# State-space stage with one chained step-size product, a tap and the masks on ScalarE, normalisation scaling inside the loop, and the first drive on VectorE

## The reference

```python
x = jnp.einsum('ed,bld->bel', in_proj_w, hidden_states)       # 256 channels, from ctx_1024
xc = conv(pad(x, 3), conv_w)                                  # 4 taps along the tokens, per channel
u = jax.nn.silu(xc + conv_b[None, :, None])
x_dbl = jnp.einsum('ke,bel->bkl', x_proj_w, u)
dt_lo, Bm, Cm = x_dbl[:, :8], x_dbl[:, 8:24], x_dbl[:, 24:]
delta = jax.nn.softplus(jnp.einsum('er,brl->bel', dt_proj_w, dt_lo) + dt_proj_b[None, :, None])
A = -jnp.exp(A_log)                                           # 256 channels x 16 states
def step(state, xs):
    dA = jnp.exp(d_t[..., None] * A)
    state = state * dA + (d_t * u_t)[..., None] * B_t[:, None, :]
    return state, jnp.einsum('ben,bn->be', state, C_t)
y = (scan(step) + D[None, :, None] * u) * jax.nn.silu(z)      # z = layernorm(x)
x = x + jnp.tanh(g_xattn[0]) * y
```

## Time and profile before

| what | us |
|---|---|
| median of three runs | 1066.79 |
| the profiled execution, its own time | 1067.51 |
| its span | 1065.8 |
| first convolution instruction on VectorE | 12.00 |
| B rows sent to DRAM (line 275); first row DMA back (line 280) issued | 29.39; 31.29 |
| first instruction of the series | 34.20 |
| delta complete; POOL's second du starts | 52.04; 52.11 |
| first scan | 56.90 |
| last product of the loop ended | 169.93 |
| last addition of the stage ended | 177.03 |
| blank tile (`blank`, a memset on POOL, line 405) set | 1.16 |

### The profile page before, as it was taken

How to read it: one execution, slowest core, us unless ns; L and a number is a source line. 1 busy time by engine, 2 the same in 40 slices (tenths; PEclk the granted TensorE clock), 3 DMA queues, 4 the chain that set the end, 5 groups by cost and what they waited for, 6 DMA issues and landing times. The chain is left out here.

```text
span 1065.8 us, 16398 instructions
## 1 busy us (share of the span) xinstructions
PE 846.5 (79%) x5192; PEld 502.3 (47%) x5198; DVE 735.5 (69%) x1433; ACT 575.6 (54%) x1095; POOL 398.9 (37%) x337
## 2 busy tenths in 40 slices
PE   3446565899999999999499588999649999925587
PEld 1112223563477777777267473333425666622235
DVE  5889998688976667666678777997361324138685
ACT  3433433468777777777366365888413433215462
POOL 0376660037655555454133163000003676310132
PEclk8679998999999999999789899999959999966589
DMA  3212202900000000000000100410194332240001
GB/s 95 81 68 71 79 20 87 347 11 2 15 20 16 20 16 20 20 15 10 6 1 1 55 1 2 141 41 2 45 333 133 78 74 46 35 114 1 0 1 40
DMA packets 44346, 57.61 MB, mean 54 GB/s; under 512 B 5672, under 2 KB 35120, under 8 KB 44288
## 3 DMA queue, kind: packets, MB, share of 16 engines
q1 hardware_dynamic: 37792, 48.72, 13.7%
q0 software_dynamic: 4416, 6.03, 3.4%
q10 hardware_dynamic: 2080, 2.10, 0.6%
HBM read 50.29 MB, written 6.49 MB: 53 GB/s over the span
## 5 line engine op out<-in xcount | busy, mean ns | idle before, releaser
L1237 POOL TENSOR_TENSOR a_scratch<-a_scratch,a_inverse 128x512 f32<-128x512 f32 x64 | 66.6, 1041 | 115.2 <-DVE a_inverse L1373 115.2
L324 PE MATMUL bank<-ssm_seen,ident 128*128 128x512 f32 x128 | 63.8, 622 | 38.8 <-DVE ssm_seen L500 38.8
L392 ACT ACTIVATE bank<-ssm_delta,ssm_a_neg 128x510 f32<-128x510 f32 x64 | 44.1, 690 | 80.7 <-DVE ssm_state L490 77.7
L426 POOL TENSOR_TENSOR ssm_drive<-ssm_du,ssm_b_row 128x1024 f32<-128x1024 f32 x32 | 75.2, 2351 | 33.4 <-DVE ssm_state L490 33.4
L2436 PE MATMUL bank<-wup,moe_xT 128*128 x184 | 83.0, 594 | 1.2 <-ACT moe_xT L2499 1.1
L2230 DVE TENSOR_REDUCE a_tops<-bank 128x4 f32<-128x1024 f32 x64 | 77.7, 1223 | 8.6 <-PE bank L1912 5.6
L490 DVE TENSOR_TENSOR_SCAN ssm_state<-bank,ssm_drive 128x512 f32<-128x512 f32 x64 | 74.8, 1210 | 7.5 <-POOL ssm_drive L426 4.9
L2671 DVE TENSOR_TENSOR moe_act_f<-bank,moe_silu 128x512 f32<-128x512 f32 x23 | 15.9, 691 | 90.9 <-ACT moe_silu L2506 79.1
L2080 ACT ACTIVATE wup<-bank,a_exp_scale 128x1024 f32<-128x1024 f32 x64 | 71.2, 1114 | 13.6 <-PE bank L1935 13.6
L1156 ACT ACTIVATE a_scratch<-bank,a_bias,a_q_factor 128x256 f32<-128x256 f32 x128 | 71.1, 560 | 7.1 <-DVE a_bias L1360 6.8
L968 PE MATMUL bank<-keys,a_scratch 128*128 (+1 forms) x256 | 69.1, 392 | 1.6 <-DVE xn L1300 0.7
(11 more groups left out here) (477 smaller groups left out, 2186.3 us busy)
## 6 DMA issues: line engine op xcount, KB each, us to landing
ssm_b_row<-ssm_b_spill SPq DMA_DIRECT2D x16, 512.0 KB, 3.6
wup<-in_l_up_dram SPq DMA_DIRECT2D x8, 1024.0 KB, 8.3
a_wq_in<-in_l1x_q_dram SPq DMA_DIRECT2D x32, 128.0 KB, 2.1
wdn<-in_l_down_dram SPq DMA_DIRECT2D x8, 512.0 KB, 9.5
keys<-in_l1x_o_dram SPq DMA_DIRECT2D x1, 2048.0 KB, 10.8
X<-in_x_dram SPq DMA_DIRECT2D x1, 1024.0 KB, 7.0
lora_raw<-in_l_gate_dram SPq DMA_DIRECT2D x1, 1024.0 KB, 8.3
lora_raw<-in_l_up_dram SPq DMA_DIRECT2D x1, 1024.0 KB, 10.3
```

The lines of the kernel that those rows point to most:

```text
L324: last = pe.matmul(bank[:, 4 + 2 * k + h, :], core.ident[:, :], seen[:, k, h * HALF:(h + 1) * HALF], start=False, stop=m >= STEPS - CC, sk ...
L426: pool.tensor_tensor(drive[:, k, :], du[:, k, :], b_row[:, n % NROW, :], ALU.mult).then_inc(S["drive_ready"], 1)
L1237: pool.tensor_tensor(prob[:, j, :, :], prob[:, j, :, :], inverse[:, j, :].unsqueeze(2).to_broadcast([P, 2, SEQ]), ALU.mult).then_inc(S["p_ ...
```

## The change

- The transposed first step-size matrix is multiplied by the second on TensorE (lines 310 and 315 of the new kernel), and the 256 x 256 product is applied to u directly (`steps_in`). 32 rows are made from u instead of 40, behind it.
- Dummy matmuls on the blank tile are placed before the first real ones and between the small ones (`keep_busy`).
- ScalarE writes the last tap straight from the bank into `ssm_conv`; VectorE adds the other three, reading the bank. `ssm_padded` is gone.
- The mask is ScalarE's Relu(1/16 - small), four bytes wide, in place of POOL's one-byte comparison.
- The C rows are spread in float32: 32-row `x_rows` by a float32 `select`, two products of two passes each. The split into parts is gone.
- The normalisation keeps its statistics ahead of the loop. Its root is exp(-0.5 log), x is centred by ScalarE inside the loop, and the scale is applied in the silu, one piece per 128 tokens.
- VectorE makes du(0) and drive(0); POOL makes du(1) and drives 1 to 31.
- The input DMAs are waited for in smaller groups, and ident and select go ahead of x. The last additions are 512 wide, four instead of eight.

The core of the diff:

```diff
-        w_dt2 = s.sb("w_dt2", [XR, CC * P])
+        w_dt2, w_xT = s.sb("w_dt2", [DR, CC * P]), s.sb("w_xT", [DR, CC * P])
+        w_c = s.sb("w_c", [P, CC, CC * P])
...
-        select3 = s.sb("select3", [96, NS * P], BF16)
-        padded = s.sb("padded", [P, CC, NB, SEQ + PAD])
+        select_in, select = s.sb("select_in", [2 * NS, NS * P], BF16), s.sb("select", [2 * NS, NS * P])
+        sixteenth, nmean, log_var = s.sb("sixteenth", [P, 1]), s.sb("nmean", [P, NT]), s.sb("log_var", [P, NT])
...
+        DT_BANK = (0, 6)
...
-                sp.dma_start(w_in[:, :], d["l0x_in"]).then_inc(S["w_s"], 16)
-                sp.dma_start(ctxT[:, :], d["ctxT"]).then_inc(S["w_s"], 16)
+                sp.dma_start(w_in[:, :], d["l0x_in"]).then_inc(S["in_s"], 16)
+                sp.dma_start(ctxT[:, :], d["ctxT"]).then_inc(S["in_s"], 16)
...
+                sp.dma_start(w_dt2[:, :], d["l0x_dt2"]).then_inc(S["w_s"], 16)
+                sp.dma_start(core.ident[:, :], d["ident"]).then_inc(S["ident_s"], 16)
+                sp.dma_start(select_in[:, :], d["select3"][0:2 * NS, NS * P:2 * NS * P]).then_inc(S["s_s"], 16)
+                sp.dma_start(core.X[:, :, :], d["x"].rearrange("(t p) d -> p t d", p=P)).then_inc(S["x_s"], 16)
...
-                pe.wait_ge(S["w_s"], 4 * 16)
-                for k in range(CC):
+                def keep_busy(n):
+                    for _ in range(n):
+                        pe.matmul(bank[:, 7, 0:DM], core.blank[:, 0:P], core.blank[:, :], start=True, stop=True)
...
+                def steps_in(o, k):
+                    for h in range(2):
+                        last = pe.matmul(bank[:, DT_BANK[o] + h, :], w_c[:, k, o * P:(o + 1) * P],
+                                         u[:, k, h * HALF:(h + 1) * HALF], start=k == 0, stop=k == CC - 1,
+                                         skip_group_check=True)
+                    if k == CC - 1:
+                        last.then_inc(S["dt_done"], 1)
+
+                pe.wait_ge(S["blank_set"], 1)
+                keep_busy(5)
+                pe.wait_ge(S["in_s"], 2 * 16)
+                for k in range(CC):
+                    in_proj(k)
+                pe.wait_ge(S["w_s"], 2 * 16)
+                pe.wait_ge(S["ident_s"], 16)
+                for k in range(CC):
+                    last = pe.transpose(bank[0:DR, 4, k * P:(k + 1) * P], w_x[:, k, 2 * NS:XR], core.ident[:, :])
+                last.then_inc(S["x_turned"], 1)
+                keep_busy(3)
+                pe.wait_ge(S["w_xT_ready"], 1)
+                for k in range(CC):
+                    last = pe.matmul(bank[:, 5, k * DM:(k + 1) * DM], w_xT[:, k * P:(k + 1) * P], w_dt2[:, :],
+                                     start=True, stop=True)
+                last.then_inc(S["chained"], 1)
+                keep_busy(4)
+                pe.wait_ge(S["w_c_ready"], 1)
+                for k in range(CC):
+                    pe.wait_ge(S["u_ready"], k + 1)
+                    for o in range(CC):
+                        steps_in(o, k)
...
+                        last = pe.matmul(bank[0:2 * NS, 4 + h, :], w_x[:, k, 0:2 * NS], u[:, k, h * HALF:(h + 1) * HALF],
                                          start=k == 0, stop=k == CC - 1)
                 last.then_inc(S["rows_done"], 1)
+                pe.wait_ge(S["diag_ready"], CC)
                 pe.wait_ge(S["rows_ready"], 1)
                 for k in range(CC):
-                    for h in range(2):
-                        last = pe.matmul(bank[:, 2 * k + h, :], w_dt2[2 * NS:XR, k * P:(k + 1) * P],
-                                         x_rows[2 * NS:XR, h * HALF:(h + 1) * HALF], start=True, stop=True)
-                    last.then_inc(S["dt2_done"], 1)
-                pe.wait_ge(S["diag_ready"], CC)
-                pe.wait_ge(S["parts_ready"], 1)
-                for k in range(CC):
+                    if k == CC - 1:
+                        pe.wait_ge(S["positive_ready"], CC)
                     for h in range(2):
                         pe.matmul(bank[:, 4 + 2 * k + h, :], skip_diag[:, k, :], u[:, k, h * HALF:(h + 1) * HALF],
                                   start=True, stop=False, skip_group_check=True)
-                pe.wait_ge(S["s_s"], 2 * 16)
-                pe.wait_ge(S["abs_done"], CC)
-                pe.wait_ge(S["positive_ready"], CC)
+                pe.wait_ge(S["select_ready"], 1)
 
                 def c_rows(n):
                     if n >= 1:
                         pe.wait_ge(S["seen_ready"], CC * n)
                     for h in range(2):
-                        last = pe.matmul(bank[:, 2 + h, :], select3[:, n * P:(n + 1) * P],
-                                         parts[:, h * HALF:(h + 1) * HALF], start=True, stop=True)
+                        last = pe.matmul(bank[:, 2 + h, :], select[:, n * P:(n + 1) * P],
+                                         x_rows[:, h * HALF:(h + 1) * HALF], start=True, stop=True)
...
+                def tap(k):
                     act.wait_ge(S["in_done"], k + 1)
-                    for h in range(2):
-                        last = act.copy(padded[:, k, 2 * h:2 * h + 2, PAD:PAD + SEQ],
-                                        bank[:, 2 * k + h, :].rearrange("p (b n) -> p b n", b=2))
-                    last.then_inc(S["pad_ready"], 1)
-                for k in range(CC):
+                    act.activation(two(conv[:, k, :]), bank[:, 2 * k:2 * k + 2, :], ACT.Identity,
+                                   scale=conv_w[:, k, TAPS - 1:TAPS]).then_inc(S["tapped"], 1)
+
+                def input_of(k):
                     act.wait_ge(S["conv_done"], k + 1)
                     act.activation(u[:, k, :], conv[:, k, :], ACT.Silu, bias=conv_b[:, k, :]).then_inc(S["u_ready"], 1)
-                act.wait_ge(S["set_up"], 2)
-                s.norm_root(act)
-                act.wait_ge(S["rows_done"], 1)
-                act.copy(two(x_rows[:, :]), bank[0:XR, 4:6, :]).then_inc(S["rows_ready"], 1)
-                act.wait_ge(S["rows_ready"], 1)
-                act.copy(parts[0:2 * NS, :], x_rows[0:2 * NS, :]).then_inc(S["parts_hi"], 1)
-                act.wait_ge(S["w_s"], 4 * 16)
+
+                act.preload_act_table_set("silu_and_others")
...
+                act.wait_ge(S["x_turned"], 1)
+                act.copy(w_xT[:, :], bank[0:DR, 4, 0:CC * P]).then_inc(S["w_xT_ready"], 1)
+                act.wait_ge(S["chained"], 1)
+                act.copy(w_c[:, :, :], bank[:, 5, :].rearrange("p (k n) -> p k n", k=CC)).then_inc(S["w_c_ready"], 1)
+                input_of(0)
+                act.wait_ge(S["s_s"], 16)
+                act.copy(select[:, :], select_in[:, :]).then_inc(S["select_ready"], 1)
+                input_of(1)
...
+                    act.activation(is_small[:, k, :], small[:, k, :], ACT.Relu, scale=-1.0, bias=sixteenth[:, 0:1]
+                                   ).then_inc(S["small_known"], 1)
...
+                for k in range(CC):
+                    exponential(k)
+                logarithm(0)
+                act.wait_ge(S["rows_done"], 1)
+                act.copy(two(x_rows[:, :]), bank[0:2 * NS, 4:6, :]).then_inc(S["rows_ready"], 1)
+                positive_part(0)
+                logarithm(1)
+                positive_part(1)
+                act.wait_ge(s.aggr_done, NT)
+                act.activation(log_var[:, :], core.meanvar[:, :, 1], ACT.Ln, bias=core.eps[:, 0:1]).then_inc(S["logged"], 1)
+                act.wait_ge(S["logged"], 1)
+                act.activation(core.rstd[:, :], log_var[:, :], ACT.Exp, scale=-0.5).then_inc(S["root"], 1)
...
+                def centre(t):
+                    act.activation(core.xn[:, t, :], core.X[:, t, :], ACT.Identity, bias=nmean[:, t:t + 1]
+                                   ).then_inc(S["centred"], 1)
+
+                act.wait_ge(S["nmean_ready"], 1)
                 for m in range(STEPS):
                     decays(m)
-                act.wait_ge(s.xn_ready, NT)
-                act.activation(silu_z[:, :, :], core.xn[:, :, :], ACT.Silu).then_inc(S["silu_z_done"], 1)
-                act.wait_ge(S["gates_s"], 2 * 16)
+                    if m >= CC * NT and m % CC == 0:
+                        centre(m // CC - NT)
+                act.preload_act_table_set("silu_and_others")
+                act.wait_ge(S["root"], 1)
+                for t in range(NT):
+                    act.wait_ge(S["centred"], t + 1)
+                    act.activation(silu_z[:, t, :], core.xn[:, t, :], ACT.Silu, scale=core.rstd[:, t:t + 1]
+                                   ).then_inc(S["silu_z_done"], 1)
...
-                for k in range(CC):
-                    pool.wait_ge(S["e_ready"], k + 1)
-                    pool.tensor_scalar(is_small[:, k, :], small[:, k, :], 1.0 / 16, None, ALU.is_lt).then_inc(S["small_known"], 1)
-                for k in range(CC):
-                    pool.wait_ge(S["delta_ready"], k + 1)
```

(30 more changed lines are left out.)

109 lines of the change are left out of this document (50 added, 59 removed).

## The result

The changed kernel took 1057.67 us, the median of 7 runs (1053.64 to 1061.38); the kernel before took 1066.79 beside it (7 runs, 1065.38 to 1071.86). The ratio is 0.989 (0.987 to 0.991). The profiled execution took 1053.64 us with a span of 1051.6, where such an execution was forecast at 1052.8 with a span near 1051.1. So the forecast of the gain held for that execution to within 0.8 us, and the median of seven fell 5.6 us short of it, 0.3 us inside the range's end at 1058.

A forecast was written before the change was run, and what follows sets the result against it. The state-space stage was bounded by an engine-hopping preparation chain, then by VectorE in the loop. Savings of 3.0 + 1.6 + 7.2 + 3.1 + 0 - 0.4 + 0.2 = 14.7 us gave 1052.1 against the 1066.79 median, range 1048 to 1058.

The forecast's parts named there:

- rivals 3 and 4: Loop: C rows late at the high level, about 1056.5, chance 0.09; preparation: TensorE low, +5 us, 1057, chance 0.07.
- Start to convolution: From kernel start to VectorE's convolution: dummies and a covered table load start it at 9.0 against 12.00, saving 3.0 us.
- rival 4: Preparation: TensorE stays at the low level and the dummies stand in the way, +5 us, 1057; chance 0.07.
- Convolution: VectorE's convolution: two multiplies leave, six multiply-adds reading a bank take 7.85 us, done at 16.85; saves 1.6 us.
- Convolution to series: Convolution's end to the step-size series: fewer passes and no copy, 5.5 us against 12.73; saves 7.2 us.
- Series: VectorE's step-size series: POOL's masks and first du leave that stretch, 3.7 us back, 0.6 us wait; saves 3.1 us.
- First drive: Series' end to the first scans: VectorE and POOL take turns on shared ports, so 0 us gained (-2.1 to +2.4).
- rival 1: First drive: ports cost more than thought, POOL goes first and VectorE's du(0) waits; minus 2.1 us, 1054.2; chance 0.13.
- rival 2: First drive: no port conflict, so the drive gain is real; +2.4 us, 1049.7; chance 0.14.
- Tail: After the loop to the stage's end: four wide additions for eight, silu pieces hidden; saves 0.2 us (-0.3 to +0.5).
- Loop: State-space loop: f32 C rows cost nothing at the high level, only the first pair runs late; -0.4 us (-1.5 to 0).
- rival 5: Loop: f32 C rows at TensorE's low level, +3.1 us per pair, +47 over 15 pairs, 1099; chance 0.03.

## Why the prediction was right or wrong

**Inside its range, short by 5 us.** 1052.1 was forecast, 1048 to 1058; the 13 runs have 1057.2. The direction and most of the mechanism held, term by term up to the first scan. That the median lies inside the range owes something to luck: it is 0.8 us from the end, and it lies near rivals 3 and 4 (1056.5 and 1057) although neither of them happened.

*Start to convolution:* 12.00 - 9.06 = 2.9 us (3.0). Without dummies 1.1 of it is lost, and 3.1 more further on, since the passes behind silu then run longer too. The run without dummies is rival 4, made real: 4.2 us, priced at 5.

*Convolution:* 7.71 us for six multiply-adds reading banks (7.85); done at 16.77, forecast 16.85.

*Convolution to series:* 22.32 - 16.77 = 5.55 us, 5.5 forecast. Undoing the product of the matrices alone costs 4.7 us of the 7.2. The rest of the term is put down to the covered table load and to the level by subtraction; the run without dummies shows that the level is worth up to 3.1 us here.

*Series:* 14.30 us long, 14.75 forecast: the wait for the positive part was 0.17, not 0.6. The four-byte mask costs next to nothing (1.37 and 1.29 us; 1.30 and 1.29 with one byte). Of the 3.7 us, putting the masks back on POOL loses 1.2 and putting du(0) back 2.0 (16.32 us long for 14.30).

*First drive:* turns, as forecast. The first scan came 4.44 us behind the series (4.8), the first product 8.92 against 61.46 - 52.04 = 9.42 before. So about +0.4 us, where 0 was said; neither rival 1 nor rival 2 happened. Taking du(1) from POOL gave 0.7 more; the two together are far from the 2.4 on paper.

*Tail:* the eight silu pieces cost nothing that a wait shows; the tail's two products wait for the last gather, as before. What comes behind the stage has the same length.

*Loop: the step that failed.* The term was -0.4, from a rule that at the high level nothing is late and that only the first pair meets the low one. The first half nearly holds: no product waits for a C row in the 128-row runs behind the first pair, only the last product is 0.35 us late. The second half is what failed. Against the low level in the loop (rival 5) the prediction argued that the stretch was granted 0.95 with TensorE 60% busy "and the change makes it busier". It did become busier, and the conclusion is wrong: the loop is 86% busy and granted 0.85. The seven profiled executions with 32-row f32 C rows and no fill took 122.2, 123.7, 127.6, 128.0, 122.2, 128.1 and (kernel before with such rows) 128.5 us for it, at 0.81 to 0.87. Those with all rows in use, 96 rows in bf16, or one bf16 pass took 120.1 to 121.0. So the loop lost 2 to 8 us by execution, the unexplained 0.5 included. The level is low in pieces, and that is why rival 5's 47 us did not come: a stretch makes a product late only if it falls on a C row or leaves TensorE behind, and the gather has time until two steps later. In the four executions near 128 us three things came together: the level rose only 12 to 13 us after the first gather had begun (after 3.5 us in the first profile), so that the first C row ran low; two of the later low stretches were 7 us long; and the last low stretch left the gathers late for the last product, which waited 1.9 to 2.5 us.

How this makes the 5 us: in the first profile the loop and its tail took 1.9 us from the forecast, the chain gave 0.8 and the later stages 0.4; with 0.3 us more outside the span that execution missed by 0.8. Both profiled executions, before and after, are ones with short later stages (888.8 and 888.4 us), so they compare like with like. The only other profile of the unedited kernel has 1.5 us more in the loop and 4.5 more behind it. The profiles of edited kernels have up to 6 more in either (888.3 to 894.8 us behind the loop). The times of the kernel before fall in two groups too (near 1066 and near 1071), and its median of 1066.79 is in the lower one, while the changed kernel's 1057.67 is 4 us above its own lower times (near 1053.6). So a part of the 5 us may well be that more of its executions had the longer later stages, whose code didn't change. How often each falls where was not measured; the split of the 5 us between the loop and the later stages stays open.

That 32-row f32 passes bring the low stretches is shown from both sides: by adding them, and little else, to the kernel before (+8.3 us in the loop, +9.1 in the median), and by adding nothing but zero rows to the changed one (clock 0.85 to 0.95). The second is the stronger, since order, number, length and spacing of the passes stay. A filler raises the level with the C rows as they are, so these need not bring it down. Why rows count, why one bf16 pass of 32 rows still leaves three low stretches, and why the low stretch at the loop's start is sometimes so long, is open.

## What to carry to other kernels

Trace the chain by hand-overs and remove engines from it: the series starts 11.9 us earlier with a projection and a copy fewer, a table load under a DMA wait, ScalarE's tap and dummy matmuls that raise TensorE's level beforehand, and each saving could be read off the timeline. Before replacing a narrow-type pass by a wider one, compare its duration at both levels with its slack, also at the loop's two ends. Don't take a busy TensorE for one that keeps its high level: here passes on 32 rows lost it, and the same passes padded with zero rows kept it. Where time is to be saved on VectorE or POOL, look at what the other one does in the same microsecond; here the saving was that of the turn, not of the instruction. And profile an unedited kernel twice before explaining 5 us: here two profiles of it differed by 6.5 us, 4.5 of them in stages that the change had not touched.

## What the runs showed of the hardware

- TensorE, busy for 86% of a loop, was granted 0.85 with f32 passes of 32 rows, and 0.95 with the same passes on 128 rows of which 96 are zero. The low stretches took 3.4 us, one of them 6.8, and most began 13.7 us after the one before.
- Matmuls of zeros raise the level too: 22 of them (44 passes of 256 columns, 9.66 us) ahead of the loop raised its granted clock from 0.96 to 1.00.
- VectorE's product of two SBUF tensors of 128x1024 takes 1.23 us alone and 3.25 beside a like one on POOL, which itself takes 3.25 instead of 2.3. Two POOL masks with one input each, 6.51 us together, stretched three multiply-adds beside them by 1.4 us in all.
- ScalarE's table load takes 1.28 us, and the next instruction starts 0.01 to 0.02 us behind it, in both kernels.
- In unchanged code two executions of one kernel differed by 4.5 us, 4.1 of them around one place where the level was low for 24 us instead of 10.
